# A four-layer megakernel: the second layer's output product in three rounded terms, its activation split between ScalarE and VectorE

## The reference, cut to what matters

```python
k = einsum('btc,oc->bto', xk, w_key)
v = einsum('btc,oc->bto', xv, w_value)
r = sigmoid(einsum('btc,oc->bto', xr, w_rec))
...
wkv = (e1 * aa_p + e2 * v) / (e1 * bb_p + e2)
return einsum('btc,oc->bto', r * wkv, w_out)      # the product that changes
...
x = x + s * g
xn = _layernorm(x)                                # then the third layer
```

## Time and profile before

| | us |
|---|---|
| median of 3 runs | 870.85 (869.34 to 871.97) |
| profiled execution, its own time | 870.72 |
| profiled execution, span | 868.9 |
| TensorE busy | 846.4 (97%) |
| VectorE busy | 632.8 (73%) |
| ScalarE busy | 473.7 (55%) |

### The profile page before, as it was taken

The page is one execution under the profiler, slowest core; times in us unless marked ns, Lnnn a source line. Parts: engine busy times, 40 slices in busy tenths (PEclk is TensorE's granted clock), DMA queues, the critical chain, the costliest instruction groups (busy, mean ns, idle before and its releaser), DMA issues.

```text
span 868.9 us, 15565 instructions
## 1 busy us (share of the span) xinstructions
PE 846.4 (97%) x5400; PEld 707.3 (81%) x5400; DVE 632.8 (73%) x1272; ACT 473.7 (55%) x944; POOL 452.7 (52%) x300
## 2 busy tenths in 40 slices
PE   7999999999999999999999999999999999999998
PEld 5888888888865899999999878778888887866688
DVE  6798989898987765664656869477667685447667
ACT  3666666666654565656643375733353435366743
POOL 5576767676623735575666021059718216608620
PEclk9999999999999999999999999999999999999999
DMA  8101010100006365546213150011111010030001
GB/s 331 37 19 36 18 36 18 36 18 21 15 0 254 102 231 191 173 165 210 77 43 91 45 206 1 1 50 49 36 36 36 13 61 1 1 146 2 3 2 49
DMA packets 23342, 62.17 MB, mean 72 GB/s; under 512 B 3136, under 2 KB 13632, under 8 KB 20224
## 3 DMA queue, kind: packets, MB, share of 16 engines
q1 hardware_dynamic: 21760, 57.35, 19.5%
q0 software_dynamic: 1536, 4.20, 1.5%
HBM read 50.00 MB, written 8.39 MB: 67 GB/s over the span
## 4 chain that ended last, share of the span: by engine, by line
PE 88%; DVE 7%; ACT 3%; issue 1%; DMA 1%; POOL 0%; SPq 0%; DVEq 0%; POOLq 0%
PE banks L101 26%; PE banks L102 25%; PE banks L103 25%; PE banks L1333 4%; PE banks L1319 2%; DVE banks L1860 1%; PE banks L990 1%; PE banks L1162 1%; PE banks L925 1%; PE banks L926 1%; DVE arenaC_rounded L1869 1%; PE banks L851 1%; PE banks L1004 1%; PE banks L968 1%; DMA arenaC<-in_wqkv 1%
## 5 line engine op out<-in xcount | busy, mean ns | idle before, releaser
L2064 ACT ACTIVATE banks<-banks,small 128x512 f32<-128x512 f32 x128 | 84.9, 663 | 79.6 <-DVE small L1467 79.6
L1467 DVE TENSOR_REDUCE small<-banks 128x1 f32<-128x512 f32 x128 | 86.8, 678 | 10.5 <-PE banks L103 10.5
L101 PE MATMUL banks<-xnT_rounded,arenaD_rounded 128*128 128x512 f32 x224 | 89.9, 401 | 3.7 <-POOL arenaC_rounded L719 2.1
L102 PE MATMUL banks<-s_tok_rounded,arenaD_rounded 128*128 128x512 f32 x224 | 90.1, 402 | 0.0
L103 PE MATMUL banks<-arenaC_rounded,arenaD_rounded 128*128 128x512 f32 (+1 forms) x256 | 89.6, 350 | 0.0
L103 PE MATMUL banks<-xnT_rounded,arenaC_rounded 128*128 128x512 f32 x192 | 76.6, 399 | 0.0
L103 PE MATMUL banks<-xnT_rounded,arenaD_rounded 128*128 128x512 f32 x192 | 75.9, 395 | 0.0
L101 PE MATMUL banks<-arenaC_rounded 128*128 128x512 f32 (+1 forms) x192 | 71.4, 372 | 1.1 <-DVE arenaC_rounded L1620 0.6
L1482 DVE SCALAR_TENSOR_TENSOR arenaC<-banks,small,arenaC 128x512 f32<-128x512 f32 x96 | 71.1, 741 | 0.0
L102 PE MATMUL banks<-arenaD_rounded,arenaC_rounded 128*128 128x512 f32 (+1 forms) x192 | 68.5, 357 | 0.0
L705 POOL TENSOR_TENSOR arenaD_rounded<-arenaC,ones 128x512 fp32r<-128x512 f32 x30 | 31.3, 1042 | 55.2 <-DVE arenaC L1482 54.2
(11 more groups left out here) (428 smaller groups left out, 2721.4 us busy)
## 6 DMA issues: line engine op xcount, KB each, us to landing
arenaD<-in_wexp SPq DMA_DIRECT2D x8, 1060.0 KB, 7.2
arenaD<-in_wexp SPq DMA_DIRECT2D x8, 1024.0 KB, 4.9
arenaC<-in_wqkv SPq DMA_DIRECT2D x16, 384.0 KB, 3.1
arenaD<-in_wexp SPq DMA_DIRECT2D x8, 512.0 KB, 3.6
slots<-arenaB SPq DMA_DIRECT2D x1, 2560.0 KB, 10.5
arenaB<-in_sw SPq DMA_DIRECT2D x1, 2084.0 KB, 7.5
arenaC<-in_wo SPq DMA_DIRECT2D x1, 2048.0 KB, 14.8
arenaC<-slots SPq DMA_DIRECT2D x8, 256.0 KB, 3.4
```

What stands on the lines that cost most here:

```text
L101: pe.matmul(o, r(lhs[0]), r(rhs[0]), start=start, stop=False)
L102: pe.matmul(o, r(lhs[0]), r(rhs[1]), start=False, stop=False)
L1467: dve.tensor_reduce(negmax[:, n % 4:n % 4 + 1], bank[3 + n % 4][:, :], AX.X, ALU.max, negate=True).then_inc(max_done, 1)
L2064: act.activation(prob[r], prob[r], ACT.Exp, bias=negmax[:, r:r + 1], accum_out=rowsum[:, r:r + 1]).then_inc(exp_done, 1)
```

## The change

`out_rows` calls `product` instead of a plain matmul. For that the output weights are split like the others: `fold(8)` copies them rounded to `w_rwkv_out_hi` and `fold_rest(8)` leaves the rest in place, now after all nine hidden tiles. The activation is split in two steps of its own: once VectorE has the product in `rr[b]`, ScalarE writes it rounded into `vv[b]` (`wkv_round`), and VectorE then subtracts that from `rr[b]` (`wkv_rest`). `rwkv_done` counts three steps for each half, and TensorE waits for the third.

```diff
--- before.py
+++ after.py
@@ -264,6 +264,7 @@
         vec = part(small, 756, 16, r="p (i c) -> p i c", i=8)
         offs = part(small, 772, 6, r="p (i c) -> p i c", i=3)
         w_rwkv_hi = part(arenaC, 5632, 3 * DC * D, r="p (i c o) -> p i c o", i=3, c=DC)
+        w_rwkv_out_hi = part(arenaC, 7168, DC * D, r="p (c o) -> p c o", c=DC)
         w_lin_hi = part(arenaD, 4168, DC * D, r="p (c o) -> p c o", c=DC)
         lin_bias_hi = part(arenaC, 5184, D)
         two_rows = part(arenaC, 5440, P)
@@ -1159,8 +1160,9 @@
 
                     b = t // ST
                     for c in range(DC):
-                        mm = pe.matmul(bank[S_BANK[1][t // 2]][:, (t % 2) * D:(t % 2 + 1) * D], rr[b][:, c, t % ST * P:(t % ST + 1) * P],
-                                       w_rwkv[:, 3, c, :], start=(c == 0), stop=(c == DC - 1))
+                        mm = product(pe, bank[S_BANK[1][t // 2]][:, (t % 2) * D:(t % 2 + 1) * D],
+                                     [m[:, c, t % ST * P:(t % ST + 1) * P] for m in (vv[b], rr[b])],
+                                     [w_rwkv_out_hi[:, c, :], w_rwkv[:, 3, c, :]], c == 0, c == DC - 1)
                     mm.then_inc(s_ready, 1)
 
                 HAD_BANK = (0, 1, 6, 7)
@@ -1193,13 +1195,14 @@
                 for t in range(ST):
                     lin_rows(t, 2 + t // 2)
                 pe.wait_ge(kr_done, 6)
-                pe.wait_ge(rwkv_done, 1)
+                pe.wait_ge(fold_split, 10)
+                pe.wait_ge(rwkv_done, 3)
                 for t in range(ST):
                     out_rows(t)
                 pe.wait_ge(kr_done, 8)
                 for t in range(ST, NT):
                     lin_rows(t, 2 + t // 2)
-                pe.wait_ge(rwkv_done, 2)
+                pe.wait_ge(rwkv_done, 6)
                 for t in range(ST, NT):
                     if t == NT - 1 and layers > 2:
                         turn_xn(2, range(ST))
@@ -1668,6 +1671,9 @@
                     i, c = (0, 2, 1)[n // 2], n % 2
                     w = w_rwkv[:, i, c, :]
                     ins = dve.scalar_tensor_tensor(r(w), w, vec[:, i, c:c + 1], rounded(w_rwkv_hi[:, i, c, :]), ALU.mult, ALU.subtract)
+                elif n == 8:
+                    w = w_rwkv[:, 3]
+                    ins = dve.tensor_tensor(r(w), w, rounded(w_rwkv_out_hi), ALU.subtract)
                 elif n == 6:
                     ins = dve.tensor_tensor(r(w_lin), w_lin, rounded(w_lin_hi), ALU.subtract)
                 else:
@@ -1694,8 +1700,7 @@
 
             for f in range(NF + 1):
                 shared_split(0, (f,))
-                if f < 8:
-                    fold_rest(f)
+                fold_rest(f)
             dve.sem_inc(fold_split, 1)
             shared_split(1, range(2))
             combine(0)
@@ -1820,13 +1825,19 @@
                     dve.wait_ge(kr_done, 4 * b + 4)
                     dve.tensor_tensor(rr[b], rr[b], vv[b], ALU.mult).then_inc(rwkv_done, 1)
 
+                def wkv_rest(b):
+                    dve.wait_ge(rwkv_done, 3 * b + 2)
+                    dve.tensor_tensor(r(rr[b]), rr[b], rounded(vv[b]), ALU.subtract).then_inc(rwkv_done, 1)
+
                 residuals(0, 1, lambda: first_key(0))
                 rests(1, 1)
                 mixed_values(0)
                 first_key(1)
                 wkv(0)
                 mixed_values(1)
+                wkv_rest(0)
                 wkv(1)
+                wkv_rest(1)
                 residuals(1, 0)
                 rests(2, 0)
                 residuals(1, 1)
@@ -2188,6 +2199,10 @@
                 if n < 6:
                     i, c = (0, 2, 1)[n // 2], n % 2
                     ins = act.activation(r(w_rwkv_hi[:, i, c, :]), w_rwkv[:, i, c, :], ACT.Copy, scale=vec[:, i, c:c + 1])
+                elif n == 8:
+                    for q in range(2):
+                        act.wait_ge(rows_out[q], ROWS0 + 32 * NE // 2)
+                    ins = act.copy(r(w_rwkv_out_hi), w_rwkv[:, 3])
                 elif n == 6:
                     act.wait_ge(bias_done, 2)
                     ins = act.copy(r(w_lin_hi), w_lin)
@@ -2206,7 +2221,7 @@
                     else:
                         ins = act.activation(bank[n % 4][:, :], bank[n % 4][:, :], ACT.Gelu)
                     ins.then_inc(shid_done, 1)
-                    if b == 0 and f < 8:
+                    if b == 0:
                         fold(f)
 
             def gate_silu(layer, quarters=range(NT // 2)):
@@ -2248,6 +2263,11 @@
                     act.wait_ge(kvr_ready, 6 * b + 2 + o + 1)
                     act.activation(rr[b][:, o, :], bank[4 + o][:, :], ACT.Sigmoid, bias=bias1[:, 2, o:o + 1]).then_inc(kr_done, 1)
 
+            def wkv_round(b):
+
+                act.wait_ge(rwkv_done, 3 * b + 1)
+                act.copy(r(vv[b]), rr[b]).then_inc(rwkv_done, 1)
+
             if layers > 1:
 
                 keys1(0)
@@ -2267,7 +2287,9 @@
                     act.copy(r(part(arenaC, 10752, DC * (768 + E2))), part(arenaC, 0, DC * (768 + E2))).then_inc(wq_rounded, 1)
                 keys1(1)
                 exponentials1(1)
+                wkv_round(0)
                 receptance(1)
+                wkv_round(1)
                 gate_silu(1)
                 turned(2, (0, 1))
```

## The result

The kernel after takes 875.93 us (median of 8 runs, 872.74 to 876.58), the kernel before 870.77 in the same comparison (8 runs, 868.86 to 872.44). The ratio is 1.0058, with a 95% interval from 1.0046 to 1.0070: 5.1 us slower, between 4.0 and 6.1. 876.1 was forecast.

What follows compares the result with a forecast made beforehand. TensorE, busy 97% of the span, bounds the kernel, level with VectorE's chain at `qkv_rows`. 870.72 plus 4.3 for the chain gives 875.0, plus 1.1 for the clock 876.1 us; range 873.8 to 878.0.

Steps and rivals of the forecast that it cites:

- TensorE's own work: `out_rows`: 6.76 us of float32 passes become 5.64 us, 1.1 us less, which falls inside the new wait and is worth nothing.
- The step of 0.1175 us: `out_rows` on TensorE: each of the 48 rounded matmuls of 256 columns takes 0.1175 us, as in `lin_rows`.
- Weight split at 0: Shared expert's stage: ScalarE's copy (about 0.6 us) and VectorE's subtraction (about 0.7) are covered and cost 0.
- First wait of 2.0 us: TensorE before `out_rows`: a new wait of 2.0 us for VectorE's rest of the first batch.
- The chain, +4.4 us at the residual: VectorE, second batch: `residuals(1, 0)` starts near 531.5 instead of 527.11, through two rests, a rounding and the late SiLU.
- The last term: VectorE before the residual: the SiLU ends after the second rest and adds 0.65 to 0.75 us.
- `qkv_rows` +4.3 us: Third layer's first projection on TensorE: starts at 539.5 to 539.6 instead of 535.26, and nothing behind gives it back.
- The wait of 2.8 us before the transposes: TensorE before the eight transposes: idle from 534.35 to about 537.1 for the normalised tiles.
- The clock, +1.1 us: TensorE after the wait before the transposes: a lower clock loses nothing to 1.7 us, taken as 1.1; chance 0.6.
- The sign that I had named for it: TensorE: a granted clock below 1.00 within the 4 us behind the transposes.
- the rival named worse: Clock falls at the first wait of 2.0 us too, or stays down for a second stretch: 878 to 880; chance 0.02.
- The low end of the range: Whole kernel: 873.8 us, the wait without the clock and runs spreading 1.5 us below their median.

Runs made afterwards that it cites:

- e1: Kernel after without the activation split: VectorE writes the product rounded, both activation operands are that tensor; 869.85 us, ratio 0.9999 against the kernel before.
- e2: Kernel after with all of the split work kept, but `out_rows` again one float32 matmul per half of the channels; 875.82 us, ratio 1.0060 against the kernel before.
- e12: Kernel after run once more, unchanged; 875.5 us, ratio 1.0068 against the kernel before.
- e3: Kernel after with activation split and three terms for the first half of the tokens only; 872.11 us, ratio 1.0027 against the kernel before.
- e7: Kernel after with unread matmuls in TensorE's two waits, 16 before `out_rows` and 12 before the transposes; 874.43 us, ratio 1.0052 against the kernel before.
- e4: Kernel after with activation split and three terms for the second half of the tokens only; 874.19 us, ratio 1.0052 against the kernel before.
- e5: Kernel after with the SiLU of tiles 0 to 3 ahead of ScalarE's second rounding; 873.79 us, ratio 1.0037 against the kernel before.
- e6: As e5, with VectorE's second rest moved between the residuals of tiles 0, 1 and 2, 3; 872.69 us, ratio 1.0039 against the kernel before.
- e11: Three terms for the second half of the tokens only, as e10 but with e8's ScalarE order; 870.58 us, ratio 1.0009 against the kernel before.
- e8: As e6, with ScalarE rounding the next layer's weights ahead of `receptance(0)`; 870.92 us, ratio 1.0012 against the kernel before.
- e9: Kernel before with GpSimd's subtraction on the third layer's weights held back until VectorE's second-half first key; 871.41 us, ratio 1.0023.
- e10: Three terms for the second half of the tokens only, e6's order, GpSimd held back as in e9; 871.60 us, ratio 1.0026 against the kernel before.

## Why the prediction was right, point by point

- *TensorE's own work is less and worth nothing.* Shown by e1 (ratio 0.9999 with the short product and no activation split) and e2 (1.0060 with the split and no short product; `qkv_rows` after 19.81 us against 19.74 in e12). The step of 0.1175 us was measured as 0.118 at the full clock.
- *Weight split at 0.* e1 has it, and its time is that of before within 0.9 us.
- *First wait of 2.0 us:* 2.10. That it is slack is right for the whole change, though not in itself: with the first half alone it sets the end (e3).
- *The chain, +4.4 us at the residual:* +4.67. First rest 1.15 (1.26 forecast), rounding with its hand-over 1.11 (1.10), second rest 1.23 (1.27), SiLU 1.10 (0.65 to 0.75). The last term was mis-sized: I let VectorE start 0.60 us after the SiLU's start, and it started 1.05 after it (528.83 and 529.88), and as late in e2, e7 and e12; in e4 it was 0.69. Why it differs was not settled. e4 measures the second half's share as 3.16, e5 the SiLU's place as 1.14.
- *`qkv_rows` +4.3 us:* +4.49 in the first profile, and +4.53 at the third layer's gate: nothing behind gave it back.
- *The wait of 2.8 us before the transposes:* 2.99 in e12, where the clock was up before it; 1.45 in the first profile, where the clock had fallen on `out_rows`.
- *The clock, +1.1 us:* 0 in the first profile at this place and 1.40 in e12. The sign that I had named for it, a clock below 1.00 within 4 us behind the transposes, is in e12 and not in the first profile. It falls in one place or the other, in every profile of the kernel after that I have (two). 4.53 and 5.93 us stand beside the 5.1 us of the medians. That 875.93 lies 0.2 us from 876.1 is in part luck: the chain was 0.2 longer than the sum, the clock term is a mean of two outcomes, and the falls near 10 and 780 us, which come and go between executions of the same code there, move single executions by 1.9 and 0.6 us.
- *A step that failed, in the rival named worse:* a fall at the first wait was given 0.02 and priced as a loss. It came in the first profile, and it was the cheap case, since it lay on work that had slack. In e6, where the slack is gone, the same fall made TensorE about 0.5 us late. The kernel before held the sign of it: its own fall near 10 us begins behind an idle bracket as long as this wait, though there TensorE had been idle for most of the time before it as well.

```profile
10.26 0.51 PE L101 MATMUL banks<-xnT_rounded,arenaD_rounded 128*128 128x512 f32 x1 [2.09 <-POOL arenaC_rounded L719]
```

- *That the waits bring the fall* is supported by a count. Seven profiles have an unfilled wait of 2 us or more in this stretch, and the clock fell behind a wait in five of them (the kernel after, e12, e2, e4, e6) and not in e3 and e5. In the seven without one (the kernel before, e1, e7 to e11; the longest wait is 1.50 us) it fell in none. So a wait makes it possible and not certain. An idle bracket is not the only thing that comes before a fall: near 448 us the kernel before falls to 0.50 with no idle time on TensorE, after 24 matmuls of one column (444.25 to 446.98). What it takes was not measured.
- *The low end of the range:* 875.0 less the 1.5 us that are named for it is 873.5, not 873.8. Nothing hangs on it here.

## What to carry to other kernels

Before a product is made cheaper, read which chain ends last at the next point where the engines meet. Here TensorE and VectorE were level within 0.15 us, so work taken from TensorE brought 0.2 us (e1), and the 4.7 us put on VectorE's chain cost 4.5. A hand-over to a second engine and back costs more than its instruction: here the rounding of 1.05 us made VectorE idle for 1.11 and pushed a table load out of its cover, another 1.10. And new idle time on TensorE is not free even where it is slack, since the clock may fall behind it: for nothing in the first profile, for 1.40 us in e12. Last, a single profiled execution carries falls of the clock from elsewhere, so compare a stretch with the same stretch and not the two times.

## What the runs showed of the hardware that was not expected

Some elementwise work of GpSimd and VectorE did not run side by side. A VectorE instruction of two elements in each lane took 2.14 us beside a GpSimd subtraction of 3.55 us and 0.16 us without it (e8); a product of 1.22 us took 4.46 us (e9, also in e10), while GpSimd's own grew from 3.55 to 4.38 when VectorE was at work at its start. In each case the later one seemed to wait until the earlier was over; that is inferred from where they end. It does not hold for every pair. The VectorE instructions that were held up read both operands from tiles such as `small` and `arenaB`. Those that read one operand from `banks`, where TensorE's products land, kept their length beside GpSimd's: all 32 of the next form take 0.70 us. Kernel before, third layer:

```profile
577.21 2.41 POOL L659 TENSOR_TENSOR arenaB<-arenaB,con 128x1024 f32<-128x1024 f32 x1
578.68 0.70 DVE L1860 TENSOR_TENSOR banks<-banks,arenaC 128x512 f32<-128x512 f32 x1 [1.84 <-PE banks L103]
579.29 0.68 DVE L1869 TENSOR_TENSOR arenaC_rounded<-banks,arenaD_rounded 128x512 fp32r<-128x512 f32 x1
```

So a GpSimd instruction that reads such tiles should stand where VectorE is idle or reads from `banks`. To hold it back to where VectorE was busy made the kernel before 0.2% slower (e9).
